# Window attention's query convolution as nine products over four shifted copies, and the FFN residuals added on VectorE

## The reference

```
x1 = xp + bn(dwconv3x3(xp))                 # dw0
x2 = x1 + bn(W2 relu(bn(W1 x1)))            # first FFN
x3 = x2 + window_attention(x2)              # windows of 7 x 7, 25 of them
x4 = x3 + bn(dwconv3x3(x3))                 # dw1
y  = x + x4 + bn(W2' relu(bn(W1' x4)))      # second FFN, and the block's input

def cga(window):                            # 4 heads, 16-wide queries and keys, 32-wide values
    q, k, val = split(bn(per-head 1x1 projection))
    q = bn(dwconv(q, qdw_w, pad=2))         # 5 x 5, one filter per channel
    attn = softmax(q @ k * 0.25 + bias)
    return proj(relu(val @ attn))
```

## Time and profile before

| | us |
|---|---|
| median of 3 runs (4018.17 to 4033.24) | 4029.28 |
| the profiled execution's own time | 4038.93 |
| its span in the trace | 4036.1 |
| first store of y, last store of y in the trace | 187.4, 1119.7 |
| steady turn of the convolution phase (store to store) | 64.5 |

### The profile page before, as it was taken

The page is one execution under the profiler, slowest core; times in us unless marked ns, Lnnn a source line. Parts: engine busy times, 40 slices in busy tenths (PEclk is TensorE's granted clock), DMA queues, the critical chain, the costliest instruction groups (busy, mean ns, idle before and its releaser), DMA issues. The chain is left out here.

```text
span 4036.1 us, 74325 instructions
## 1 busy us (share of the span) xinstructions
PE 3284.0 (81%) x26644; PEld 2560.8 (63%) x26644; DVE 2924.7 (72%) x5398; ACT 2212.4 (55%) x3456; POOL 737.9 (18%) x869
## 2 busy tenths in 40 slices
PE   5889898888756568888888888888888886699993
PEld 3566565656445446767766776776767675587872
DVE  7898989998634357767777777787777775577763
ACT  2545545554334346656666666666656663477770
POOL 1000000000000100122122121122121122466660
PEclk9999999999877779988898888899889997899995
DMA  1223131322347599999999999999999994577768
GB/s 50 92 75 121 68 121 68 126 83 97 117 144 290 215 314 363 353 319 342 338 348 344 327 345 334 334 371 332 341 324 332 357 335 150 189 243 238 237 203 333
DMA packets 278691, 980.15 MB, mean 243 GB/s; under 512 B 47524, under 2 KB 53424, under 8 KB 269286
## 3 DMA queue, kind: packets, MB, share of 16 engines
q1 hardware_dynamic: 261094, 942.17, 65.5%
q0 software_dynamic: 17280, 33.87, 2.3%
HBM read 486.23 MB, written 489.85 MB: 242 GB/s over the span
## 5 line engine op out<-in xcount | busy, mean ns | idle before, releaser
L1094 DVE CUSTOM_DVE_ANT_0 att_skewed<-att_score_ps,att_skewed 128x1024 f32<-128x1024 f32 x512 | 625.4, 1222 | 271.7 <-issue 254.2
L956 ACT ACTIVATE att_skewed<-att_skewed,att_neg_max 128x1024 f32<-128x1024 f32 x512 | 588.8, 1150 | 350.8 <-DVE att_neg_max L1094 350.0
L1212 PE MATMUL att_turn_ps<-att_ident,att_skewed 128*128 128x128 f32 x4096 | 594.6, 292 | 110.1 <-ACT att_skewed L956 107.8
L947 ACT ACTIVATE att_rows<-att_wide_ps 128x1152 f32<-128x1152 f32 x512 | 574.1, 1121 | 184.1 <-PE att_wide_ps L1176 182.8
L1212 PEld LDWEIGHTS att_turn_ps<-att_ident,att_skewed 128*128 128x128 f32 x4096 | 497.9, 150 | 278.3 <-ACT att_skewed L956 239.9
L1102 DVE COPY att_turned<-att_turn_ps 128x1024 f32<-128x1024 f32 x512 | 625.2, 1221 | 30.8 <-PE att_turn_ps L1212 30.2
L1176 PE MATMUL att_wide_ps<-att_ps,att_qs 98*128 98x128 f32 (+3 forms) x1920 | 456.8, 361 | 52.6 <-issue 30.1
L1204 PE MATMUL att_score_ps<-att_ks,att_qs 96*128 96x512 f32 x1024 | 382.9, 457 | 21.2 <-DVE att_neg_max L1094 20.1
L1176 PEld LDWEIGHTS att_wide_ps<-att_ps,att_qs 98*128 98x128 f32 x1920 | 327.2, 210 | 108.4 <-issue 66.5
L911 POOL DMA_INDIRECT expert_rows<-att_expert_rows,att_place x256 | 247.1, 965 | 792.0 <-DVE att_place L1052 706.5
L152 POOL DMA_INDIRECT expert_parts<-exp_parts,exp_rows x284 | 300.1, 1057 | 195.2 <-ACT exp_parts L183 129.2
(11 more groups left out here) (258 smaller groups left out, 5529.6 us busy)
## 6 DMA issues: line engine op xcount, KB each, us to landing
skewed_rows<-att_rows SPq DMA_DIRECT2D x512, 576.0 KB, 5.4
att_skewed<-skewed_rows SPq DMA_DIRECT2D x512, 512.0 KB, 7.1
expert_rows<-conv_pad SPq DMA_DIRECT2D x144, 520.0 KB, 7.0
exp_weights<-split_weights SPq DMA_DIRECT2D x71, 1028.0 KB, 6.8
att_qs<-queries SPq DMA_DIRECT2D x192, 128.0 KB
att_ks<-keys SPq DMA_DIRECT2D x192, 128.0 KB
exp_rows<-expert_rows SPq DMA_DIRECT2D x71, 260.0 KB, 2.8
sum_part<-expert_parts SPq DMA_DIRECT2D x32, 512.0 KB, 9.7
```

What stands on the lines that cost most here:

```text
L947: act.activation(rows[s % ROWS][:], wide_ps[:, 0:WIDE], ACT.Copy).then_inc(wide_read, 1)
L956: act.activation(skewed[r % RING][:], skewed[r % RING][:], ACT.Exp, bias=neg_max[:, k:k + 1], scale=-1.0, accum_out=sums[:, k:k + 1]).then ...
L1094: dve.tensor_tensor_reduce(skewed[r % RING][:], score_ps[:], skewed[r % RING][:], -SCALE, 3.0e38, ALU.add, ALU.min, neg_max[:, k:k + 1]).t ...
L1212: last = pe.transpose(turn_ps[:, t * P:(t + 1) * P], skewed[r % RING][:, t * P:(t + 1) * P], ident[:])
```

## The change

Queries' convolution. The 25 taps all go to PE. For each quarter a of the channels (32 of them), `stacked[:, a]` holds four copies of that quarter of `qp` on the four quarters of the partitions: unshifted, shifted by one column, by one row, and by both. A product over all 128 partitions with a 128 x 32 matrix then does four taps at once for 32 channels, so that nine passes cover 25 taps (with zeros for the 11 that don't exist). Sixteen DMAs from SBUF to SBUF an image make the copies, issued by SP. DVE's 14 instructions and four additions go; ACT empties the four tiles into `q` with the bias (`convolved`).

FFNs. The identity products go. DVE empties the FFN's last tile with `(tile + shift) + x1` into `branch` (`end_first`), or with `(tile + shift) + y` into `y` after `y = x4 + xo` (`end_last`). ACT copies `branch` straight into windows and separately keeps it in `x2`.

Order. Queries, keys and convolution of an image move into the turn before it, the last 3x3 convolution of image n to the end of turn n, the first FFN of image n+2 to the end of PE's turn n, and the second FFN's of image n-1 ahead of the turned weights.

```diff
-QTAPS_PE = 11
+PASSES = 9
@@ SP
+            def copies(n):
+                used(sp, place(n, "Q"))
+                for k, offset in enumerate((0, 1, WS + 4, WS + 5)):
+                    for a in range(4):
+                        to = stacked[k * DH:(k + 1) * DH, a, :, :].rearrange("p r c -> p (r c)")
+                        of = flat(qp[a * DH:(a + 1) * DH, :, :])
+                        size = (SLOTS * PITCH + 4) * (WS + 4) - offset
+                        sp.dma_start(to[:, 0:size], of[:, offset:offset + size]).then_inc(copied, 16)
...
                 if not (isinstance(n, int) and n >= NB - 3):
                     sp.wait_ge(xp_ready, n + 3)
                     sp.dma_start(x[:], x_dram[n + 3]).then_inc(x_loaded, 16)
+                if not is_last(n):
+                    copies(n + 1)
                 if not is_first(n):
                     store(n - 1)
@@ ACT
+            def convolved(n):
+                for j in range(4):
+                    at = place(n, f"C{j}")
+                    filled(act, at)
+                    part = slice(4 * j * QROW, min(4 * j + 4, SLOTS) * QROW)
+                    act.activation(q[:, part], tile[at[0]][:, 0:part.stop - part.start], ACT.Identity,
+                                   bias=col(shift, "qdw")).then_inc(tile_used[at[0]], 1)
@@ DVE
+            def end_first(n):
+                at = place(n, "F0c")
+                filled(dve, at)
...
+                dve.scalar_tensor_tensor(branch[:], tile[at[0]][:], col(shift, "ffn0_out"), x1[:], ALU.add, ALU.add).then_inc(tile_used[at[0]], 1)
+
+            def end_last(n):
...
+                sum_chain.step(dve.tensor_tensor(y[:], x4[:], xo[:], ALU.add))
+                filled(dve, at)
+                dve.scalar_tensor_tensor(y[:], tile[at[0]][:], col(shift, "ffn1_out"), y[:], ALU.add, ALU.add).then_inc(tile_used[at[0]], 1)
...
-                used(dve, place(n, "Q"))
-                convolve(qconv_chain, n, q[:, 0:SLOTS * QROW].rearrange("p (r c) -> p r c", c=WS), qp, qtaps[:], 5,
-                         SLOTS * PITCH, WS, "qdw", None)
...
-                    last_convolution(n - 1)
+                    end_last(n - 1)
                 if has_after_next(n):
-                    first_convolution(n + 2, lambda: add_attention(n))
-                else:
-                    add_attention(n)
+                    first_convolution(n + 2)
+                add_attention(n)
+                last_convolution(n)
@@ PE
                 for c in (0, HALF):
                     for j in range(2):
-                        pe.matmul(to[:, c:c + HALF], w_out[:, number, j, :], hidden[:, j, c:c + HALF], start=(j == 0), stop=False)
-                    for j, same in enumerate(carried):
-                        last = pe.matmul(to[:, c:c + HALF], ident[:], same[:, c:c + HALF], start=False, stop=(j == len(carried) - 1))
+                        last = pe.matmul(to[:, c:c + HALF], w_out[:, number, j, :], hidden[:, j, c:c + HALF], start=(j == 0), stop=(j == 1))
...
+            def convolution(n):
+                pe.wait_ge(copied, 256 * n + 256)
                 for j in range(4):
                     at = place(n, f"C{j}")
                     to = begin(at)
                     rows, end = 4 * j * PITCH, min(4 * j + 4, SLOTS) * PITCH
-                    for t in range(QTAPS_PE):
-                        dy, dx = divmod(25 - QTAPS_PE + t, 5)
-                        last = pe.matmul(to[:, 0:(end - rows) * WS], tap_products[:, t, :], qp[:, rows + dy:end + dy, dx:dx + WS],
-                                         start=(t == 0), stop=(t == QTAPS_PE - 1))
+                    for t in range(PASSES):
+                        dy, dx = (2 * k for k in divmod(t, 3))
+                        for a in range(4):
+                            last = pe.matmul(to[a * DH:(a + 1) * DH, 0:(end - rows) * WS], tap_products[:, t, a, :],
+                                             stacked[:, a, rows + dy:end + dy, dx:dx + WS], start=(t == 0), stop=(t == PASSES - 1),
+                                             skip_group_check=True)
```

More of the change, by code:

```diff
@@ L1368, in has_after_next @@
             return not (isinstance(n, int) and n >= NB - 2)
-        def items_of(n):
-            left_out = (F1 if is_first(n) else []) + (F0 if is_last(n) else []) + ([] if has_after_next(n) else ["G"])
-            return [m for m in main_items if m not in left_out]
         def place(n, item):
[L1377 to L1380, removed]
-            else:
[L1382 to L1390, removed]
+            if isinstance(n, int):
+                return number[item, n] % NT, number[item, n] // NT
+            at = number[item, 1 + ahead[item]]
+            return at % NT, PER_TURN * n + (at // NT - PER_TURN * (1 + ahead[item]))
         def image_loop(eng, prologue, turn, epilogue):
@@ L1422, in filled @@
             eng.wait_ge(tile_filled[where[0]], where[1] + 1)
[L1424 to L1432, removed]
         @block.sync
@@ L1508, in into_windows, with keep_branch, ffn @@
             def into_windows(n):
-                used(act, prepared(n, "F0c"))
+                used(act, place(n, "F0c"))
+                for row in range(NW):
+                    k = min(WS, SIDE - row * WS)
+                    lines = image(branch)[:, row * WS:row * WS + k, :]
+                    inside = lines[:, :, 0:(NW - 1) * WS].rearrange("p r (w c) -> p w r c", w=NW - 1)
+                    act.activation(xw[:, row * NW:row * NW + NW - 1, 0:k * WS].rearrange("p w (r c) -> p w r c", r=k), inside, ACT.Copy)
+                    border = xw[:, row * NW + NW - 1, :].rearrange("p (r c) -> p r c", r=WS)[:, 0:k, 0:SIDE - (NW - 1) * WS]
+                    ins = act.activation(border, lines[:, :, (NW - 1) * WS:], ACT.Copy)
+                ins.then_inc(xw_ready, 1)
+            def keep_branch(n):
                 if not is_first(n):
                     act.wait_ge(x3_ready, n)
[L1513 to L1520, removed]
+                act.activation(x2[:], branch[:], ACT.Copy).then_inc(x2_ready, 1)
+            def ffn(n, number, out, parts="abc"):
                 for j, item in enumerate("abc"):
@@ L1535, in ffn0, with ffn1, queries @@
                     act.wait_ge(x2_ready, n)
[L1536 to L1543, removed]
+                ffn(n, 0, branch, "ab")
+            def ffn1(n):
+                ffn(n, 1, y, "ab")
+                filled(act, place(n, "F1c"))
+            def queries(n):
                 at = place(n, "Q")
@@ L1603, in prologue @@
                 into_windows(0)
-            image_loop(act, prologue, turn, lambda: ffn1(NB - 1, "abc"))
+                queries(0)
+                keys_of(0)
+                convolved(0)
+                keep_branch(0)
+                ffn0(1)
+            image_loop(act, prologue, turn, lambda: ffn1(NB - 1))
         @block.vector
@@ L1722, in turn @@
             def turn(n):
+                if not is_last(n):
+                    end_first(n + 1)
                 if has_after_next(n):
                     moments_of(n + 2)
[L1725 to L1732 removed]
@@ L1776, in prologue @@
                 group_norm(1)
+                end_first(0)
                 first_convolution(1)
-            image_loop(dve, prologue, turn, lambda: last_convolution(NB - 1))
+            image_loop(dve, prologue, turn, lambda: end_last(NB - 1))
         @block.tensor
@@ L1995, in conv_layout @@
             qtaps[at] = qdw[h]
+    of_qdw = bn[:, :, BN.index("qdw")]
+    tap_sets = np.zeros((C, 9, 4), np.float32)
+    for a in range(4):
+        bn[:, :, BN.index(f"qdw_quarter{a}")] = np.tile(of_qdw[a * dv:(a + 1) * dv], (4, 1))
+        for k, (dy, dx) in enumerate(((0, 0), (0, 1), (1, 0), (1, 1))):
+            for t in range(9):
+                row, column = 2 * (t // 3) + dy, 2 * (t % 3) + dx
+                if row < 5 and column < 5:
+                    tap_sets[k * dv:(k + 1) * dv, t, a] = qtaps[a * dv:(a + 1) * dv, 5 * row + column]
     taps = np.stack([get("dw0_w").reshape(C, 9), get("dw1_w").reshape(C, 9)], 1)
```

194 lines of the change are left out of this document (116 added, 78 removed).

## The result

The changed kernel takes 4040.0 us (median of 8 runs, 4033.0 to 4043.8), the kernel before 4030.0 us beside it (4018.2 to 4039.4): ratio 1.0029 with a 95% interval of 1.0015 to 1.0043. So it is 0.3% slower, where 0.5% faster was forecast; the 10 us are less than the 20 us that I had called distinguishable, but the interval leaves out a ratio of 1. The profiled execution took 4039.0 us, its span is 4037.1.

What follows compares the result with a forecast made beforehand. DVE and PE were taken as nearly full, then a ring of 63.4 us a turn instead of 64.9: 19 - 11 x 1.5 - 21 = -18.5 us, so 4011 against the median 4029.3, range 3970 to 4075.

Steps and rivals of the forecast that it cites:

- a ring: Seven steps of a convolution-phase turn, each waiting for the one before: 61.2 us, with half clock and signals 63.4.
- Step 1: Group norm to copies complete: 14.3 us, from 3.4 for the load of x and 11.5 for sixteen copies, less overlap.
- Step 2: The queries' convolution on PE, 216 products over 252 columns and 72 over 63: 14.3 us.
- step 3: First FFN on PE: 3.6 in, 1.3 waiting for ACT, 3.4 out without the identity products, 8.3 us.
- 5 ScalarE to the windows: ACT finishes the first values' copy, then second values, windows and borders: 4.9 us, with PE idle for 5.
- 6 queries, group mean, half clock: PE's queries and group-mean product, 2.4 us with signals, plus 2.0 for queries at half clock every turn.
- 7 DVE to the norm: DVE's small group steps, softmax sums and products, group norm and signals: 9.1 us.
- the rule that I gave 7%: Rival: 32 partitions get at most about 218 GB/s, a set takes 12.5 us, turn 1.0 longer, 4026 us; 7%.
- The rival "copies slow": Gain gone at 0.8 us a copy; 4048 us with issue at 0.88, 4075 at 1 us each; 19%.
- Copies hidden: Rival: copies at 0.55 us or less, or beginning sooner, take 2.6 us off each turn, 3975 us; 20%.
- Start and end: First store of y 19 us later, near 206; twelfth store to the last 197 us instead of 218.3, -21.
- Column groups: Four run at once in the convolution; rival: only two at a time, convolution 28 us, total 4220; 5%.

Runs made afterwards that it cites:

- experiment 1: Changed kernel with the sixteen copies issued ahead of the wait for the group norm and the load of x: 3948.7 us, ratio 0.979.
- 3: Changed kernel with only eight of the sixteen copies made, two shifts' taps left out of the result: 3947.4 us.
- 2: Changed kernel with the same sixteen copies ordered so that successive ones write and read alternating halves of the partitions: 3998.3 us, ratio 0.991.
- 5: Changed kernel with four useless 512-column products in each of PE's two waits, before the queries and before the convolution: 3991.0 us, ratio 0.990.
- 8: Changed kernel with the FFNs' residuals as identity products on PE again and DVE's three passes gone: 4054.2 us, ratio 1.005.
- 12: Kernel of experiment 1 with the FFNs' residuals as identity products on PE again: 4027.2 us, ratio 1.000.
- 6: Kernel of experiment 1 with the last FFN's two input products of the image before put ahead of the queries on PE: 3944.1 us.
- 9: Kernel of experiment 6 with ScalarE writing the first hidden half before the queries and the second before the second exponentials: 3932.5 us.
- the tenth: Kernel of experiment 9 with the convolution's last quarter put between the first FFN's input and output products on PE: 3911.3 us, ratio 0.970.
- 7: Changed kernel with the written half alternating at every copy while eight in a row read one half: 4027.5 us, ratio 0.999.

## Why the prediction was wrong

The mechanism was right: a ring from group norm through copies, convolution, first FFN, scores, values, windows, queries and group-mean product back to the norm, with DVE idle in two places. Two of its terms were too small, and they sit in every turn: the turn is 3.25 us longer than forecast, which eleven times is 35.8 us, against 35.1 between the forecast of the phase (-18.5) and what it did (+16.6). The turn from the norm at 591.64 to that at 658.14, step by step as the prediction numbered them:

| step | forecast | measured |
|---|---|---|
| 1 norm to copies complete | 14.3 | 17.5 |
| 2 convolution | 14.3 | 15.0 (mean 15.5) |
| 3 first FFN | 8.3 | 8.7 |
| 4 scores and values | 7.9 | 7.3 |
| 5 ScalarE to the windows | 4.9 | 4.5 |
| 6 queries, group mean, half clock | 2.4 + 2.0 | 4.8 |
| 7 DVE to the norm | 9.1 | 8.7 |
| signals | 0.2 | - |
| sum | 63.4 | 66.5 |

- **Step 1 failed, by 3.2 us a turn.** I took 238 GB/s from the earlier trace rows for transfers of 32 partitions. Eight copies in a row that write to one half of the partitions ran at 206: 13.65 us for a set, not 11.5, which is 2.1 of the 3.2. The other 1.1 us: the first packet came 3.0 us after the norm and PE began 0.9 us after the last, where I had 3.4 less an overlap of 0.6. Moving the copies (experiment 1), halving them (3) or alternating them (2) gave 91, 93 and 42 us. The Trainium skill ("SBUF — State Buffer", "Door 1: The DMA port swizzle") has the rule that I gave 7%: each half of the partitions has half of the ports, at most about 218 GB/s. The trace agrees for eight writes in a row to one half, 206; the 245 in alternation is above that figure. My reason to set the rule aside, that the earlier trace rows lie above it, was no reason: those transfers (L814 and L834 of the kernel before) write the first, second and third quarter of the partitions in turn, never more than two in a row to one half. The rule alone gave +1.0 a turn, a third of the miss.
- **The rival "copies slow" named the right place and the wrong cause.** The sign that I had named for it, a set over 13 us, came true. The copies' 13.65/16 = 0.85 us each is beyond its break-even of 0.8, and its sum (4048) is nearer than mine. But issuing did not grow with the bytes: 10.4 to 10.7 us for sixteen, 0.66 each. The transfers were what was late.
- **Step 2: half clock came a second time.** I wrote that the turned weights to keys end 2.6 us before the copies are in, and let that idle time cost nothing. It was 4.8 us, and the convolution behind it began at half clock: 15.5 us and not the 13.5 of experiments 1, 5, 8 and 12. The forecast 14.3 for the products themselves was 0.8 too high: the 252-column ones took 12.43/216 = 58 ns each against 56 assumed, the 72 short ones 17 ns against 31.
- **The residuals.** Right that six products of 0.86 leave PE; I booked them in the work, not on the ring, except in step 3. As long as PE waits for the copies they are nearly free (experiment 8), and without that wait 5.0 us a turn (12).
- **Copies hidden** was a rival at 3975: made true by experiments 1 and 3 it gave 3949 and 3947. The turn became 59.9 where the rival's was 60.8, with the queries still at half clock as forecast; and the first store came at 186.7 and 183.7 instead of near 206, which I had not seen.
- **Start and end** held within 4 us: +15.4 for +19, -18.0 for -21. That the two misses cancel is luck. Column groups do run four at once (58 ns against some 223 for a full-width instruction over as many columns); the ring does close.

In the sum, 15.4 + 11 x 1.75 - 18.0 = +16.6 us in the phase against a forecast of -18.5; the runs' medians show +10, and the 7 us between lie within the scatter of what follows the phase.

## What to carry to other kernels

When a change takes work off full engines but puts a transfer between them, write down the ring that it closes and price the transfer by rows of the same partitions in the same order; then ask whether it can start before the thing it is queued behind. Here that one reordering turned +10 us into -83. A wait that PE gets new can be paid twice, as here: once as idle time and once as half clock behind it. So fill it with work that stands ready, and look at once for where the wait goes next: experiments 6 and 9 found it moved to another engine, and the tenth still had a part of it.

## What was not expected of the hardware

- Transfers of 32 partitions: 206 GB/s with eight writes in a row to one half, 245 when both sides alternate, 414 over 128 partitions, each with the DMA engines' share at 1. Copies to one half landed 0.84 us apart, also where the quarter changed; with the written half alternating 0.67 to 0.69, whether or not the read half alternated (experiments 2 and 7).
- Waits of 3.8 to 5.0 us left the convolution's first microseconds at half clock. In experiments 2, 5 and 8, behind waits of up to 1.9 us it took 13.4 to 13.5 us, and behind 2.1 to 3.2 us 14.7 to 15.1 (first image and the next one aside). The wait's length alone doesn't settle it: behind 2.28 us the output products of experiment 9 ran at full clock. 3.5 us of useless products in each of two waits of 4.5 and 4.8 us bought back 3.8 us a turn.
- A product of 128 x 32 over 63 columns took 17 ns in a run of 72 (1.24 us), somewhat over a quarter of the 58 ns over 252 columns.
